# Gated cross attention with an integer-rounded feed-forward: stack rows interleaved, VectorE's maxima moved ahead in four slots, scores, maxima and shift rows placed one slot earlier

## The reference, cut to what matters

```python
def attention(query, ctx):                     # 32 batches, 256 rows, 16 heads of 16 dims
    q, k, v = proj(query, Wq, bq), proj(ctx, Wk, bk), proj(ctx, Wv, bv)
    q = q * cos + rotate_half(q) * sin         # k alike
    scores = einsum('bhqd,bhkd->bhqk', q, k) / sqrt(16)
    scores = where(abs(i - j) <= 50, scores, -1e9)
    return (softmax(scores) @ v) @ Wo.T + bo
x = x + tanh(g_xattn) * attention(layernorm(x), ctx)
x = x + tanh(g_ffn) * ffn(layernorm(x))        # ffn: every operand rounded by a scale over the whole tensor
```

## Time and profile before

| | us |
|---|---|
| median of 3 runs | 1368.02 (1367.55 to 1368.43) |
| the profiled execution's own time | 1368.83 |
| its span in the profile | 1367.1 |
| DVE busy in 400 to 500 us (attention) | 94.6 of 100 |
| PE busy in the same stretch | 88.7 of 100 |
| ACT, POOL busy in the same stretch | 60.9, 72.7 of 100 |

### The profile page before, as it was taken

The page is one execution under the profiler, slowest core; times in us unless marked ns, Lnnn a source line. Parts: engine busy times, 40 slices in busy tenths (PEclk is TensorE's granted clock), DMA queues, the critical chain, the costliest instruction groups (busy, mean ns, idle before and its releaser), DMA issues. The chain is left out here.

```text
span 1367.1 us, 27802 instructions
## 1 busy us (share of the span) xinstructions
PE 1203.8 (88%) x8963; PEld 786.5 (58%) x8995; DVE 1212.9 (89%) x3603; ACT 826.5 (60%) x1336; POOL 549.5 (40%) x1357
## 2 busy tenths in 40 slices
PE   5689898989998988998988659998999799968998
PEld 3457666666666666666666434443433334427887
DVE  3799999999999999999998849997999989988886
ACT  2255656666666665656565536665677599983332
POOL 1177777777777777777776610000000000000000
PEclk9699999999999999999999869999999999988999
DMA  2757575757565666666664202223455455546764
GB/s 78 156 121 183 135 174 139 168 139 164 143 161 146 158 151 153 154 151 158 146 161 112 102 8 93 111 97 127 158 183 185 159 191 196 199 165 205 241 225 169
DMA packets 132369, 207.27 MB, mean 152 GB/s; under 512 B 11159, under 2 KB 97050, under 8 KB 126106
## 3 DMA queue, kind: packets, MB, share of 16 engines
q1 hardware_dynamic: 132250, 205.86, 54.4%
HBM read 125.60 MB, written 79.69 MB: 150 GB/s over the span
## 5 line engine op out<-in xcount | busy, mean ns | idle before, releaser
L670 DVE CUSTOM_DVE_ANT_0 psum<-psum,band 128x178 f32<-128x178 f32 x1024 | 316.5, 372 | 38.4 <-PE psum L878 38.1
L552 ACT ACTIVATE probs<-psum 128x356 f32<-128x356 f32 x512 | 210.6, 468 | 162.7 <-PE psum L895 162.2
L486 POOL TENSOR_SCALAR_AFFINE_SELECT probs<-probs 128x154 f32<-128x154 f32 (+1 forms) x512 | 221.4, 443 | 156.5 <-ACT probs L552 150.5
L1088 PE MATMUL psum<-xnT,w_upT 128*128 (+1 forms) x1152 | 261.1, 384 | 19.0 <-DVE maxima L1312 8.8
L1088 PEld LDWEIGHTS psum<-xnT,w_upT 128*128 128x128 f16 x1152 | 109.9, 99 | 170.0 <-issue 32.6
L878 PE MATMUL psum<-k_stack,q_stack 96*128 96x178 bf16 x1024 | 141.3, 245 | 51.3 <-DVE smax L670 47.4
L495 POOL TENSOR_SCALAR_AFFINE_SELECT probs<-probs 128x254 f32<-128x254 f32 (+1 forms) x512 | 180.3, 375 | 0.0
L895 PE MATMUL psum<-q_stack,k_stack 98*128 98x178 bf16 x1024 | 136.2, 242 | 16.8 <-DMA q_stack<-shiftT 10.5
L670 DVE DVE_READ_ACCUMULATOR2_ANT smax<- 128x1 f32 x1024 | 142.9, 140 | 0.0
L1688 PE MATMUL psum<-w_downT,xnT 128*128 128x256 f16 x1152 | 128.3, 275 | 16.0 <-DVE xnT L1638 16.0
L878 PEld LDWEIGHTS psum<-k_stack,q_stack 96*128 96x128 bf16 x1024 | 74.2, 98 | 109.0 <-DVE smax L670 87.2
(11 more groups left out here) (189 smaller groups left out, 2265.3 us busy)
## 6 DMA issues: line engine op xcount, KB each, us to landing
k_parts_scratch<-k_parts SPq DMA_DIRECT2D x32, 384.0 KB, 2.5
q_parts_scratch<-q_parts SPq DMA_DIRECT2D x32, 384.0 KB, 2.6
k_stack<-k_parts_scratch SPq DMA_DIRECT2D x32, 384.0 KB, 5.1
q_stack<-q_parts_scratch SPq DMA_DIRECT2D x32, 384.0 KB, 7.3
gate_scratch<-g_stage SPq DMA_DIRECT2D x16, 768.0 KB, 3.2
g_in<-gate_scratch SPq DMA_DIRECT2D x16, 768.0 KB, 4.6
sig_scratch<-w_gateT SPq DMA_DIRECT2D x32, 384.0 KB, 2.3
sig_again<-sig_scratch SPq DMA_DIRECT2D x32, 384.0 KB, 3.4
```

What stands on the lines that cost most here:

```text
L486: nc.gpsimd.affine_select(out=t[:, :, 0:n], in_=t[:, :, 0:n], pattern=[[0, 2], [1, n]], compare_op=ALU.is_ge, fill=0.0, base=WINDOW - off, ...
L552: nc.scalar.activation(ring_tile(probs, b, pair, c)[:].rearrange("p e j -> p (e j)"), scoreT_bank[c][:, 0:2 * SPAN], ACT.Exp, scale=DK ** ...
L670: ins = nc.vector.tensor_tensor_reduce(out=mine, in0=mine, in1=keep["band"][:, t, :], scale=1.0, scalar=-3e38, op0=ALU.add, op1=ALU.max, a ...
L1088: last = nc.tensor.matmul(bank[:], weights[wp][:, c * I + f * P:c * I + (f + 1) * P], x_parts[:, c, bass.ds(j * (2 * TILE) + xp * TILE, TI ...
```

## The change

1. The three groups of a stack go to alternating partitions: group 0 to 0, 2, ..., 94, group 1 to 33, 35, ..., 95, group 2 to 1, 3, ..., 31. Q and K are placed alike, so each product stays the same.
2. `S_FIRST` is 10 and not 11: a batch's scores and maxima start in slot 2 of the next iteration.
3. The shift rows follow: the second half in slot 2 and not 3, the first half in slot 6 and not 7, on DVE, PE and ACT; PE waits for `divide` of b3 before it writes the first half's rows.
4. DVE takes the maxima ahead of `rope q` (slot 3), of `remainder k` (slot 4), of `low k` (slot 5, where `remainder q` stays ahead), of `low q` (slot 6) and of `statistics` (slot 7).
5. ACT copies V in slot 4, before that slot's exps and behind `high q`, and not in slot 5; the two `middle` parts come behind their slot's exps.
6. POOL's `scale_of` for x moves from slot 7 to slot 0 of the next iteration.
7. SP issues the first half's shift rows ahead of the Q stack's loads.

```diff
+GROUP_ROWS = ((0, 6 * DK), (2 * DK + 1, 6 * DK), (1, 2 * DK))
-        S_FIRST, ST_FIRST, PV_FIRST = 11, 18, 20
+        S_FIRST, ST_FIRST, PV_FIRST = 10, 18, 20
@@ SP
-                for g in range(3):
-                    rows = (3 - g) * DK
-                    sp.dma_start(stack[row:row + rows, :, :]...)
-                    row += rows
+                for g, (first, end) in enumerate(GROUP_ROWS):
+                    sp.dma_start(stack[first:end:2, :, :]...)
                 load_stacks(Batch(rnd, unit, 0), "k")
+                load_shift(Batch(rnd, unit, 1), 0)
                 load_stacks(Batch(rnd, unit, 0), "q")
-                load_shift(Batch(rnd, unit, 1), 0)
@@ POOL
-                    if slot == 7:
-                        scale_of(Batch(rnd, unit, -1), ...)
+                    if slot == 0:
+                        scale_of(Batch(rnd, unit, 0), ...)
@@ ACT
                     if slot == 3:
+                        shift_copy(b2, 1)
                         high(b0, "k")
                     if slot == 4:
-                        shift_copy(b2, 1)
                         copy_outT(b3, 1)
-                        middle(b0, "k")
                         high(b0, "q")
-                    if slot == 5:
                         ... copy of V ...
-                        middle(b0, "q")
                     if slot == 7:
                         ... copy of attT ...
+                        shift_copy(b1, 0)
                     exps(Batch(rnd, unit, late), pair)
+                    if slot == 4:
+                        middle(b0, "k")
+                    if slot == 5:
+                        middle(b0, "q")
-                    if slot == 7:
-                        shift_copy(b1, 0)
@@ DVE
                     if slot == 2:
+                        shift_parts(b2, 1)
                         rope(b0, "k", bank_b)
+                    if slot == 5:
+                        remainder(b0, "q")
+                    if slot == 6:
+                        shift_parts(b1, 0)
+                    pair, late = pair_at(slot, S_FIRST)
+                    maxima(Batch(rnd, unit, late), pair)
                     if slot == 3:
-                        shift_parts(b2, 1)
                         rope(b0, "q", bank_a)
                     if slot == 4:
                         remainder(b0, "k")
                     if slot == 5:
                         low(b0, "k")
-                        remainder(b0, "q")
                     if slot == 6:
                         low(b0, "q")
-                    if slot == 7:
-                        shift_parts(b1, 0)
-                        ... statistics(nxt) ...
-                    pair, late = pair_at(slot, S_FIRST)
-                    maxima(Batch(rnd, unit, late), pair)
+                    if slot == 7 and nxt.real:
+                        ... statistics(nxt) ...
@@ PE
-                    if slot == 3:
+                    if slot == 2:
                         ... wait for out_normed of b3, half 0 ...
                         shift_rows(b2, 1)
-                    if slot == 7:
+                    if slot == 6:
+                        if b3.real:
+                            reached(pe, out_normed, b3, HALVES, 2)
                         shift_rows(b1, 0)
```

More of the change, by code:

```diff
@@ L409, in load_stacks @@
                 reached(sp, scoredT, b.before(NBUF), 2 * PAIRS, 2 * PAIRS)
-                row = 0
-                for g in range(3):
-                    rows = (3 - g) * DK
-                    sp.dma_start(stack[row:row + rows, :, :].rearrange("r s t -> r (s t)"), scratch[n + "_rows"](b.buf, g)).then_inc(stack_loaded[n][b.buf], 16)
-                    row += rows
+                for g, (first, end) in enumerate(GROUP_ROWS):
+                    sp.dma_start(stack[first:end:2, :, :].rearrange("r s t -> r (s t)"), scratch[n + "_rows"](b.buf, g))\
+                        .then_inc(stack_loaded[n][b.buf], 16)
             def load_shift(b, half):
@@ L500, in steps @@
                 for slot in range(SLOTS):
-                    if slot == 7:
-                        scale_of(Batch(rnd, unit, -1), moments_taken, scale_steps, scale_ready, moments, scale_small, scale)
+                    if slot == 0:
+                        scale_of(Batch(rnd, unit, 0), moments_taken, scale_steps, scale_ready, moments, scale_small, scale)
                     if slot == 2:
@@ L800, in steps @@
                         low(b0, "k")
-                        remainder(b0, "q")
                     if slot == 6:
                         low(b0, "q")
-                    if slot == 7:
-                        shift_parts(b1, 0)
-                        if nxt.real:
-                            reached(dve, x_loaded, nxt, 16, 16)
-                            statistics(nxt, x_in, stats, moments, stats_taken, moments_taken)
-                    pair, late = pair_at(slot, S_FIRST)
-                    maxima(Batch(rnd, unit, late), pair)
+                    if slot == 7 and nxt.real:
+                        reached(dve, x_loaded, nxt, 16, 16)
+                        statistics(nxt, x_in, stats, moments, stats_taken, moments_taken)
                     if slot == 5:
```

## The result

The changed kernel takes 1408.9 us (median of 4 runs, 1405.2 to 1419.1), the kernel before beside it 1368.2 (4 runs, 1367.6 to 1373.2): 1.0305 times as long, 95% interval 1.0277 to 1.0333. The forecast was 1363, and its rival "the stack comes late" is what happened, at more than its price. The profiled execution is the longest of the four, 1419.1 us; its span is 50.2 us above the span of before. All ratios and intervals leave out two slow runs, e5's of 1418.6 us and e12's of 1985.1.

A forecast was written before the change was run, and what follows sets the result against it. The prediction took the loop through ACT and PE, 22.3 us, as the bound, with SP's 22.15 hidden: about 29 iterations from 22.48 to 22.3 give -5.2 us, hence 1363 us (forecast's own range 1357 to 1367, over the cases 1344 to 1392).

The forecast's parts named there:

- the stack comes late: Rival, chance 0.36: from X = 8.55 the SP loop sets the iteration, 1 us for 1; X = 9.3 gives 1385.
- X: q store's issue to the q stack's last landing: group 0 at 3.8 + 3.4, two more 0.6 each, 8.4 us.
- the loop through SP: Store, stack loads, slot 2's scores, back to the store: 8.4 + 3.1 + 10.65 = 22.15 us, just hidden below 22.3.
- the engines' loop: ACT's chain to attT's copy, PE's Wo projection, next slot 0's maxima: 17.7 + 0.9 + 3.74 = 22.3 us an iteration.
- The long issues: SP's issues, now and then up to 1681 ns against 580, in six of 27 iterations; the old 1.2 us hid them.
- lower bound of 7.8: Least X for the q stack if only issues and the shortest landing count: 3.8 + 1.2 + 2.8 us.
- the estimate of 8.7: X by the skill's port rate of about 27 GB/s: 1.2 + 0.6 + 0.6 us of data plus the old k group's landing cost.
- M: Start of slot 0's maxima on DVE, from which all times in an iteration are counted.
- break-even at 8.55: X for the q stack from which the SP loop sets the iteration; the forecast's margin to it was 0.15 us.
- DVE's stall at the k remainder: DVE's port wait during POOL's addition of the q halves: forecast to fall from 0.88 to 0.2 us.
- Slots at the start: within 1: Slots at the start and in the tail, outside the full iterations, were to change the time by at most 1 us.
- the rival's 1385: Late-stack rival's time at X = 9.3: iteration 23.05 us, 29 x 0.57 = +16 us; rival's chance 0.36.

The follow-up runs named there:

- e5: Changed kernel with PE computing half of the V projection twice on the same values: ratio 1.0244 to before, median 1412.6 us.
- e12: e2 with the shift rows' DMA ahead of the q stack's loads: 1363.8 us, ratio 0.9967 to before.
- e1: Changed kernel with the stack groups back on contiguous partitions: 1536.7 us, ratio 1.1221 to before.
- e3: Changed kernel with scores from slot 3 again (old S_FIRST), shift rows in their old slots and SP's old order: 1364.4 us, ratio 0.9972 to before.
- e7: e3 with ACT's high q moved behind slot 4's V copy and exps: 1367.9 us, ratio 0.9985 to before.
- e11: e7 with the shift rows' DMA ahead of the q stack's loads again: 1361.1 us, ratio 0.9945 to before.
- e6: Changed kernel with DVE's low q ahead of slot 6's maxima, as before the change: 1409.1 us, ratio 1.0293 to before.
- e2: Kernel before with only the stack rows interleaved over alternate partitions: ratio 0.9966 to before, iteration 22.49 us.
- e4: Changed kernel with the first half's shift rows issued behind the q stack's loads again: 1403.8 us, ratio 1.0264 to before.
- e10: e9 with the shift rows' DMA behind the q stack's loads again: 1387.9 us, ratio 1.0150 to before.
- e9: e6 and e5 together, on the changed kernel: 1384.2 us, ratio 1.0118 to before.

## Why the prediction was wrong

**The step that failed** is the sum X = 8.4 from the q store's issue to the last landing, in the terms for the landing: group 0 at 3.4 after its issue, the other two 0.6 later each. I took the 3.4 from a load over all partitions and gave it no spread. The runs show a mean X of 9.8, so the loop through SP takes 23.5 us and sets the iteration, where I had it hidden below the engines' loop:

- The issues were right: the q loads go out 3.89 behind the store (3.8 forecast), the third of them 1.25 later.
- Each group lands about 4 us after its own issue, whatever its size: 4.0, 4.0 and 4.2 in the median. My sum has the last group at 3.4 after its own issue. The steps of 0.6 nearly came out (0.6 and 0.8), but from the spacing of the issues and not from the bytes that I had given as the reason. With the medians, and 0.1 to PE's start, it is 3.89 + 1.25 + 4.2 + 0.1 = 9.4.
- In the iterations that wait, slot 2's scores come 9.1 to 11.3 behind the store, 10.2 in the median, since in most of them either an issue is late or the last landing long: 128 KB take up to 6.1.
- In nine of the 27 iterations an issue on SP is long, and the last q issue ends 6.7 to 7.4 behind the store, not 5.7 to 6.2. In seven of them the q store itself lands only 4.1 to 4.9 after its issue, not 2.5 to 2.7, and the first q load goes out 4.7 to 5.5 behind it. These seven hold 12.2 of the 27.5 us. In the one of 597.49 the three k loads took 3.50 us where they take 1.87, and the store 4.8:

```profile
593.57 0.37 SPq L402 DMA_DIRECT2D q_parts_scratch<-q_parts  x1
594.03 3.50 SPq L412 DMA_DIRECT2D k_stack<-k_parts_scratch  x3
...
q_parts_scratch<-q_parts SPq DMA_DIRECT2D x1, 384.0 KB, 4.8
```

The long issues I had named as a risk and priced nowhere, and the store I had landing at 2.6 always. The mean of X over the iterations was what counted, and its spread is all on one side. The lower bound of 7.8 was out of reach by the same error, as it took 2.8 for the landing that comes last; the shortest one of q's last group is 3.4. The Trainium skill ("SBUF — State Buffer", "Door 1: The DMA port swizzle") had the direction right, as e1 against the changed kernel shows (7.0 to 4.2 for the last q group); the estimate of 8.7 that I made from it adds to 8.9 by its own terms: the old group's landing of 5.1 less 2.4 of data (an estimate by the page's port rate, as are the 1.2 + 0.6 + 0.6) gives 3.8 + 2.7 + 2.4. That puts group 0's landing at 3.9, where 4.0 was measured, nearer than my 3.4; the spread it doesn't have either.

**The loop's other terms held.** The store goes out at 522.91 = M+18.58 (forecast 18.55), and the loop is X + 13.7 (forecast 3.1 + 10.65 = 13.75): 9.74 + 13.7 = 23.4 for the iteration of 526.84, measured 23.42. The rival's line "1 us for 1" is so confirmed, and by it the 27.5 us of waits follow from X. With the break-even at 8.55 (8.8, as the traces have it, since the engine loop is 22.5), the rival needed a mean X of some 9.8 (8.8 and 27.5 / 27); it was priced with 9.3, and the forecast with 8.4.

**The engines' loop**, forecast 22.3, is 22.5 in the changed kernel and 22.35 in e3. Here the order of the working was right: DVE's wait ahead of slot 0 stays at 0.99, ACT sets the pace, and taking high q out of the way (e7, e11) gives 0.17 back. DVE's stall at the k remainder is gone, as forecast (829 ns in the mean, some 0.9 us forecast, 1492 ns before), though 0.16 us of it come back at the q remainder (942 ns against 785), and so is PE's wait for the shift rows.

**What I priced at nothing:** PE's clock. Its waits in slots 5 and 6, 1.17 for the exps and 0.45 for xn, lie beside other work and cost nothing as waits, but the clock can fall behind them: 9.3 us in this execution, with 3.4 more behind waits for the stack, and 0.88 us in each of 24 iterations of e6. So the rival's engine loop would not have been 22.3 in each iteration even with a stack in time.

**"Slots at the start: within 1"** was wrong by 9 us. At the start nothing else is there to hide the load, and a slot earlier makes PE wait where it waited 2.96 us before. The loss is larger than the 9.6 shows, for interleaving alone gains 5.6 there (e2). PE's waits in the first 100 us of the changed kernel:

```profile
48.31 0.75 PE L878 MATMUL psum<-k_stack,q_stack 96*128 96x178 bf16 x4 [7.30 <-DMA q_stack<-q_parts_scratch]
71.86 0.75 PE L878 MATMUL psum<-k_stack,q_stack 96*128 96x178 bf16 x4 [1.48 <-DMA q_stack<-q_parts_scratch]
96.43 0.75 PE L878 MATMUL psum<-k_stack,q_stack 96*128 96x178 bf16 x4 [3.25 <-issue]
```

The three add to 12.0; less 2.96 it is 9.1 of the 9.6 us.

So the rival's 1385 would have needed two more terms, the clock (12.8) and the start (9.6), and a longer X (27.5 us of waits and no gain on the engines, where it had 16 us in all), to come to the 1419 of the profiled execution. The 1409 of the median has less of one or more of them, and no trace tells of which.

Open is why a q load issued earlier takes longer to land (e4, e10, and e2 and e3 with 4.9 to 5.4, where it also follows k's loads at once). It isn't the wait for the q store, since SP issues these loads only when that has landed; that they share the queues with k's groups is a guess. Open is also why the q store lands late and issues on SP take 1 to 2 us longer in the same iterations. Neither was tried.

## What to carry to other kernels

When a change takes slack out of a transfer, write the chain as issue, plus issue, plus the last transfer's own landing in full, and take the landing's spread and not its median: what arrives late lengthens the iteration by all of it, what arrives early gives nothing back. A transfer made faster should first be run without using up what it gives (e2), and only then be asked for earlier, by no more than the slowest landing leaves. And a wait of TensorE beside other work is not free if its clock falls behind it; look at the granted clock of the stretch that follows (e6 against e9).

## What the runs showed of the hardware

- In the changed kernel a load into the stack, its rows spread over alternate partitions, lands 4.0 to 4.3 us after its issue in the median, at 384, 256 and 128 KB alike; contiguous (e1), q's loads take 6.1 to 7.0 and k's 5.1 to 5.8.
- Issued 1.33 us earlier behind the store of what they read, q's loads take 4.8 to 5.4 from issue to landing (e4), 5.1 to 5.6 in e10: the landing hardly moves.
- In 7 of 27 iterations of the changed kernel the q store of 384 KB took 4.1 to 4.9 us to land, not 2.5 to 2.7; in the same seven SP's three issues of k's loads took 2.7 to 3.5 us together, not 1.9.
- TensorE went to its 1.2 GHz level behind idle times as short as 1.17 and 0.45 us, in five of the changed kernel's 27 iterations (granted clock 0.50 from 495 to 499 us, 0.69 until 503) and in the first 24 of e6's; in the others it stayed at 2.4 GHz behind the same idle times. With half a projection more ahead of them the idle times were 0.30 and 0.46 us, no fall followed in any iteration (e9), and the kernel was faster by doing more: 1384.2 us against e6's 1409.1.
